# Four adj products and a W2 product in 128-wide tiles; three of the adj passes and the W2 product rewritten as one level of Strassen's seven products

## What is computed

```
def _gc(x, adj, W, b):
    return adj @ (x @ W) + b
h = jnp.maximum(_layernorm(x, axis=-1), 0.0)
h = jax.nn.relu(_gc(h, adj, W1, b1))
h = jax.nn.relu(_gc(h, adj, W2, b2))
return x + _gc(h, adj, W3, b3)
```

## Time and profile before

| | us |
|---|---|
| median of 3 runs (1734.08 to 1735.21) | 1734.35 |
| span of the profiled execution, from its first to its last instruction | 1732.1 |
| TensorE busy (matmul) | 1717.0 (99%) |
| VectorE busy | 628.4 (36%) |
| ScalarE busy | 451.6 (26%) |
| GpSimd busy | 43.8 (3%) |
| mean DMA rate | 110 GB/s |

### The profile page before, as it was taken

How to read it: one execution, slowest core, us unless ns; L and a number is a source line. 1 busy time by engine, 2 the same in 40 slices (tenths; PEclk the granted TensorE clock), 3 DMA queues, 4 the chain that set the end, 5 groups by cost and what they waited for, 6 DMA issues and landing times.

```text
span 1732.1 us, 23105 instructions
## 1 busy us (share of the span) xinstructions
PE 1717.0 (99%) x8352; PEld 1480.0 (85%) x8352; DVE 628.4 (36%) x1040; ACT 451.6 (26%) x829; POOL 43.8 (3%) x115
## 2 busy tenths in 40 slices
PE   7999999999999999999999999999999999999999
PEld 6788889988888899888888899888898888888899
DVE  7623333463332333653233353222233332333232
ACT  6522222332221222332222242111012322222221
POOL 6400000000000000000000000000000000000000
PEclk9999999999999999999999999999999999999999
DMA  5633333024443342133344365332253324444342
GB/s 187 190 94 102 97 97 83 9 62 119 124 116 105 107 128 70 32 105 113 108 121 120 100 188 146 95 96 85 84 154 106 98 87 136 143 147 122 105 123 86
DMA packets 133485, 190.17 MB, mean 110 GB/s; under 512 B 14938, under 2 KB 64698, under 8 KB 133422
## 3 DMA queue, kind: packets, MB, share of 16 engines
q1 hardware_dynamic: 99450, 161.39, 32.5%
q10 hardware_dynamic: 33972, 27.98, 4.9%
HBM read 161.34 MB, written 27.73 MB: 109 GB/s over the span
## 4 chain that ended last, share of the span: by engine, by line
PE 96%; DMA 1%; DVE 1%; POOL 1%; ACT 1%; issue 0%; ACTq 0%; DVEq 0%; SPq 0%
PE ps L867 32%; PE ps L868 32%; PE ps L869 32%; DMA stage<-x 1%; PE ps L891 1%; DVE stats L712 0%; DVE still_lo L543 0%; POOL spread L835 0%; POOL spread L833 0%; POOL spread L843 0%; DVE slot_lo L551 0%; ACT stage L678 0%; ACT still_hi L506 0%; ACT slot_hi L530 0%; DVE moments L714 0%
## 5 line engine op out<-in xcount | busy, mean ns | idle before, releaser
L867 PE MATMUL ps<-slot_hi,still_hi 128*128 128x512 f32 (+2 forms) x2016 | 735.1, 365 | 11.4 <-DVE still_lo L543 11.4
L868 PE MATMUL ps<-slot_lo,still_hi 128*128 128x512 f32 (+2 forms) x2016 | 734.3, 364 | 0.0
L869 PE MATMUL ps<-slot_hi,still_lo 128*128 128x512 f32 (+2 forms) x2016 | 734.0, 364 | 0.0
L551 DVE TENSOR_TENSOR slot_lo<-raw,slot_hi 128x512 fp32r<-128x512 f32 (+2 forms) x588 | 362.8, 631 | 752.0 <-ACT slot_hi L530 751.5
L530 ACT CAST slot_hi<-raw 128x512 fp32r<-128x512 f32 (+2 forms) x588 | 328.5, 573 | 1056.5 <-PE ps L869 784.1
L867 PEld LDWEIGHTS ps<-slot_hi,still_hi 128*128 128x128 f32 x2016 | 379.8, 188 | 65.4 <-DVE still_lo L543 12.4
L868 PEld LDWEIGHTS ps<-slot_lo,still_hi 128*128 128x128 f32 x2016 | 379.9, 188 | 53.0
L869 PEld LDWEIGHTS ps<-slot_hi,still_lo 128*128 128x128 f32 x2016 | 379.6, 188 | 53.1
L867 PE MATMUL ps<-W_hi,slot_hi 128*128 128x512 f32 x336 | 132.1, 393 | 0.0
L868 PE MATMUL ps<-W_lo,slot_hi 128*128 128x512 f32 x336 | 132.1, 393 | 0.0
L869 PE MATMUL ps<-W_hi,slot_lo 128*128 128x512 f32 x336 | 132.1, 393 | 0.0
(11 more groups left out here) (63 smaller groups left out, 563.4 us busy)
## 6 DMA issues: line engine op xcount, KB each, us to landing
raw<-adjT SPq DMA_DIRECT2D x336, 256.0 KB, 2.7
raw<-adjT SPq DMA_DIRECT2D x84, 192.0 KB, 2.4
raw<-adjT SPq DMA_DIRECT2D x84, 138.0 KB, 2.1
raw<-H SPq DMA_DIRECT2D x42, 256.0 KB, 2.9
raw<-W SPq DMA_DIRECT2D x32, 256.0 KB, 3.1
P<-stage ACTq DMA_DIRECT2D x32, 256.0 KB, 2.1
raw<-P SPq DMA_DIRECT2D x32, 256.0 KB, 2.7
H<-stage ACTq DMA_DIRECT2D x32, 256.0 KB, 2.3
```

Source lines behind the costliest of these rows:

```text
L551: dve.tensor_tensor(lo, src, hi.bitcast(F32), ALU.subtract).then_inc(lo_done, 1)
L867: pe.matmul(out, st_hi, mv_hi, start=start, stop=False)
L868: pe.matmul(out, st_hi, mv_lo, start=False, stop=False)
L869: return pe.matmul(out, st_lo, mv_hi, start=False, stop=stop)
```

## The change

The kernel is written anew; what is computed is the same. Its parts:

1. **Strassen.** `pass2a`, `pass2b`, `pass3` and `w2` each become one level of Strassen's scheme (seven products of half-size matrices in place of eight). For adj, 20 of the 21 full row blocks are paired (t, t + 10; `PAIRS` = 10) and the columns are split in halves of 1356 (`HALF`). The block 20 and the short one stay outside the scheme and are added as ordinary products (`left`, `slot_tail`). One group is one of the seven products (`part` 0 to 6), or the left-over one (`None`), for one chunk: ten moving tiles, each multiplied by two stationary column blocks, 6 matmuls a tile.
2. **Width.** The padded 2712 columns are 2 halves of 3 chunks of 452 (`W` = 452). `pass1` stays an ordinary product, in 3 chunks of 2 x 452 columns, over eight PSUM banks.
3. **Combined moving operands.** Four of the seven products need sums of adj blocks (T1 to T4). GpSimd makes them during `pass1` from the raw tiles, four operations per pair of tiles (`make`, L1258), 3 x 10 pairs in all, and SP stores them to DRAM (`TS`); later passes load them in place of adj. For `w2` GpSimd makes them from `P2` (`prep_moving`, L1344), with loads and stores on its own DMA queue.
4. **Combined stationary operands.** S1 to S4 are made by GpSimd from each finished pair of h1 (`combine`, L1297) for `pass2a` and `pass3`; for `pass2b` and `w2` GpSimd makes them from DRAM during `pass2a` (`prep_stationary`, L1321).
5. **Reloading.** All stationary operands (10 pairs x 7 parts) fill one array `S`. h1's second half goes to DRAM (`H1B`), and `S` is loaded and cut again for `pass2b` and for `w2` while the pass before is running: one 128 x 256 tile beside each moving tile, through the same raw buffers.
6. **Drains.** PSUM banks are added into SBUF sums (`parts`) by VectorE, 2 to 4 additions a group; ScalarE copies part 0.
7. **Buffers.** `RAW` and `RING` go from 7 to 5, x buffers from 4 to 3 (`XS`); `pass1` has 5 raw and 3 cut slots of 904 columns.
8. h1's two halves are made in one phase. P1 goes to DRAM and back. The final x is added by GpSimd. The code has no loops any more: TensorE's program goes from 4473 to 7670 rows.

The core of the diff:

```diff
-RING = 7
-RAW = 7
-STAGES = 4
-CHUNK_BLOCKS = (4, 4, 4, 4, 3, 2)
+PAIRS = 10
+W = 452
+CHUNKS = 3
+HALF = W * CHUNKS
+RING = 5
+RAW = 5
+XS = 3
+LAG = 5
...
+            def make(i, which):
...
+                    pool.tensor_tensor(T1_, Y12, Y11, ALU.subtract).then_inc(made_done, 1)
...
+                    pool.tensor_tensor(T3_, Y22, Y12, ALU.subtract).then_inc(made_done, 1)
...
+                    pool.tensor_tensor(T2_, Y22, T1_, ALU.subtract).then_inc(made_done, 1)
...
+                    pool.tensor_tensor(T4_, Y21, T2_, ALU.subtract).then_inc(made_done, 1)
...
+            for g_n, part in enumerate((0, 1, 2, 3, None, 4, 5, 6)):
...
+                if reload and c == CHUNKS - 1 and part is not None and part >= 2:
+                    extra = reload(part - 2, last_of)
...
+                    if half is not None and (t == here[0] if here else True):
+                        p.tails += 1
+                        g.tail = (p.tails, c, half, at["tail_freed"])
+                        at["tail_freed"] = g.done[-1]
+                        p.steps.append(("tail", g))
+                    spread_in(extra)
...
+                if n >= XS:
+                    sp.wait_ge(lo1_done, xs1[n - XS].ready)
...
+                    for m in range(2):
+                        cols = slice(m * P, (m + 1) * P)
+                        if n == 0:
+                            bank_free(g, m)
+                        end = g.left is None and n == len(g.tiles) - 1
+                        mm = three(ps[:, g.banks[m], 0:W], S[:, j.pair, j.part, 0, cols], S[:, j.pair, j.part, 1, cols],
+                                   ring[:, s, 0, 0:W], ring[:, s, 1, 0:W], start=n == 0, stop=end)
```

More of the change, by code:

```diff
@@ L37 @@
 BANK = 512
-RING = 7
-RAW = 7
-HEAD = 4
-LATE = 4
-STAGES = 4
-STEP = 32
-EPS = 1e-5
-CHUNK_BLOCKS = (4, 4, 4, 4, 3, 2)
-def chunk_of(block):
-    at = 0
-    for c, n in enumerate(CHUNK_BLOCKS):
-        at += n
-        if block < at:
-            return c
-    return len(CHUNK_BLOCKS) - 1
-class Job:
-    def __init__(self, kind, cut, chunk=0, tile=0, col=0, width=0, half=None, source=None):
+EPS = 1e-5
+STEP = 32
+PAIRS = 10
+FULL = 21
+SHORT = 21
+ORDER = (1, 2, 3, 4, 5, 6, 0, 7, 8, 9)
+EARLY = 8
@@ new lines, with __init__ @@
+BLOCKS = [b for t in ORDER for b in (t, t + PAIRS)] + [20, SHORT]
+W = 452
+CHUNKS = 3
+HALF = W * CHUNKS
+NP = 2 * HALF
+DIRECT = {0: (0, 0), 1: (1, 0), 6: (1, 1)}
+X11, X12, S2, S3, S1, X22, S4 = range(7)
+RING = 5
+RAW = 5
+RAW1 = 5
+RING1 = 3
+XS = 3
+LAG = 5
+class Tile:
+    def __init__(self, kind, cut):
+        self.kind, self.cut = kind, cut
+        self.raw = self.raw_freed = self.slot = None
+        self.block = self.part = self.pair = self.chunk = self.half = self.k = None
+        self.freed = self.place_freed = None
@@ L68, in __init__, with columns_chunk @@
+def columns_chunk(block):
+    first = block * P
+    last = min(first + P, 2 * HALF) - 1
+    return max((c % HALF) // W for c in range(first, last + 1))
+class Pass1Tile:
+    def __init__(self, kind, cut):
         self.kind, self.cut, self.ready = kind, cut, cut + 1
-        self.chunk, self.tile, self.col, self.width, self.half, self.source = chunk, tile, col, width, half, source
-        self.raw = self.raw_freed = self.tail_use = self.slot = self.acc_before = self.slot_before = None
+        self.raw = self.raw_freed = self.pair_freed = self.slot = None
+        self.freed = self.place_freed = None
+        self.chunk = self.block = self.n = self.k = self.col = None
@@ L297, in gcn_kernel @@
[L297 to L306 removed]
+        assert offset + size <= nc.sbuf_usable_end, (name, offset + size - nc.sbuf_usable_end)
@@ L367, in source_of @@
[L367 to L383 removed]
+        copied = sem("copied")
```

1986 lines of the change are left out of this document (1271 added, 715 removed).

## The result

The changed kernel takes 1772.51 us (median of 4 runs, 1769.16 to 1774.82), the one before 1734.78 us beside it; the ratio is 1.0218, with a 95% interval of 1.0202 to 1.0233. It is slower by 2.2%, where I had forecast 1657 us and given 0.05 to slower.

A forecast was written before the change was run, and what follows sets the result against it. TensorE's count of matmuls was taken to bound the kernel. From 1732.1 us, -136.5 for columns, +32 reload, +8 first chunk and +18.9 in smaller waits (2.4 + 5 + 2 + 7 + 2.5) gave 1654.5, or 1657 as measured; range 1612 to 1718.

The forecast's parts named there:

- The count of columns: TensorE's matmuls in the passes and `w2`: fewer columns to multiply would save 136.5 us in sum.
- 452 columns are 68 above 384: Matmul time at the new width, taken from a line between 384 and 512 columns: 0.2017 us.
- Costed at nothing: GpSimd's preparation queue: GpSimd's making of combined operands, taken as covered by the rest of `pass2a`; uncovered, some 6 us each.
- once a landing takes over 4.7 us, five buffers no longer cover: Raw buffers in the passes: threshold of 2.56 + 2.1 us landing time, above which TensorE waits.
- the rival of 0.05: Slower landings decide all through the passes: at 6.3 us each, 206 us more, 1863 us; chance 0.05.
- the mean rate, about doubled: Load rate in the passes: DMA engines, busy 0.36 of the time at 99 GB/s, would fit it doubled.
- The clock: TensorE's granted clock, read as 1.00 (2.4 GHz) in every stretch before; no term was given for a change.
- Reload: Stretches with a 256-column tile behind each moving one: 1.50 us a pair against 1.21, +32 us (bounds 9 and 96).
- The first chunk: Load of x no longer hides with three buffers: 5.3 us a block against 4.84, +8 us (bounds 0 and 35).
- That rival (0.24): GpSimd and VectorE shut each other out, in the first chunk and reload stretches: 1712 us; chance 0.24.
- the seams: Waits between phases and at short tiles: +2.4 us after `pass1`, +5 into `pass2a`, +2 into `pass3`, +7 at short tiles.
- The end: After the last matmul, VectorE, GpSimd's addition and the store follow one another: +2.5 us.

## Why the prediction was wrong

The forecast span was 1654.5 us, the measured one 1770.8. The 116 us, by the forecast's own steps (the differences are rounded):

| step | forecast | measured | difference |
|---|---|---|---|
| start of the first matmul | 9.5 | 10.5 | +1 |
| 5076 matmuls at 0.2017, 1536 in `pass1` | 1333.6 | 0.2067 and 0.2048: 1363.8 | +30 |
| block phases | 242.9 | 240.8 | -2 |
| first chunk, TensorE idle | 6.8 + 8 | 26.6 | +12 |
| rest of `pass1`, with the seam | 2.4 | 7.3 | +5 |
| chunks with preparation and no reload (first two of `pass2a`, second of `pass2b`) | 5 + 2.3 | 29.3 | +22 |
| three reload stretches | 32 + 2.3 | 67.5 | +33 |
| first chunk of `w2` | 0 | 5.4 | +5 |
| `pass3` | 2 + 2.3 | 8.1 | +4 |
| end, after the last matmul | 5.4 | 11.9 | +6 |

**The count of columns** (-136.5) was mis-sized: the saving is 106. The step that failed is "452 columns are 68 above 384", a straight line between two measured widths. The run with TensorE alone shows that it is the width, and not what runs beside it; the operand's place adds up to 2 ns. "TensorE: Matmul & The Clock Gate" of the Trainium skill, whose rule I had weighed (N/2.4 + 2.5 ns), gives 190.8 ns; no run here shows 452 columns under 204.

**"Costed at nothing: GpSimd's preparation queue"** is the step that failed outright. I asked only whether it would be done in time, not what its transfers and additions do to the tiles beside them. Leaving it out gives 48.6 us back, 30.2 by its transfers (5.4 of them at the end) and 18.4 by its additions. My own threshold, "once a landing takes over 4.7 us, five buffers no longer cover", was about right and was reached in part: the median landing was 4.5 to 4.7 us in the second chunk of `pass2a` (11.3 us of stalls) and 3.7 to 4.0 in the second of `pass2b` (4.2 us), against 2.8 to 3.3 without preparation. I had made it the rival of 0.05 for all passes at once; it came true in stretches. And I had taken the mean rate, about doubled, as harmless, where it was the landing time under that rate that counted.

**The clock** was a term put at nothing without a word: I had read 1.00 in every stretch before and carried it over. The stalls brought TensorE to 1.2 GHz eleven times, some 16 of the 116 us, which stand in the table with the stalls behind which they came.

**Reload** (+32, bounds 9 to 96) had the right formula and a short landing: 3.1 to 3.4 us in place of 2.56 for the moving tiles, 2.8 to 2.9 in place of 2.1. That alone makes (4.6 + 3.8) / 5 = 1.68 us a pair instead of 1.50. Without preparation the three stretches keep 49.3 us of stalls; the 18 us above are preparation's again, 6 of them by the clock, which fell four times in these stretches and, with the preparation left out, not once.

**The first chunk** (+8, bounds 0 to 35) had the right cause, that x has one buffer less, and too short a block: 5.3 us forecast, while the statistics start 6.3 us apart ((74.44 - 55.56) / 3):

```profile
55.56 0.69 DVE L1046 BATCH_NORM_STATS2 stats<-xs 128x6 f32<-128x512 f32 x1 [2.96 <-DMA xs<-x]
74.44 0.69 DVE L1046 BATCH_NORM_STATS2 stats<-xs 128x6 f32<-128x512 f32 x1 [2.61 <-DMA xs<-x]
```

What was missing is the mutual waiting of GpSimd and VectorE: 1.4 to 2.0 us for about every second cut, which takes 1.08 alone, and `lo` often at 1.63 instead of 0.75. That rival (0.24) was real in kind, and is a smaller part than the missing buffer. It also contributes in the passes, where VectorE's 452-column rows take 743 ns beside preparation against 628 alone.

**Right were** the seams: the largest single stalls are 2.8 us after `pass1` (2.4 forecast), 5.3 into `pass2a` (5), 2.5 into `pass3` (2), 0.95 at each short tile (0.78); that plain chunks stall at nothing else; and ScalarE waiting for the DMA in the reload stretches. The end was missed: not the addition, which costs 1.1 us each, but GpSimd's drain, with whose late work the tail is 6.3 us longer than without it.

The chances were wrong in their shape. Most of the mechanisms that came true stood in the text, and I let each go wrong alone. In the passes they share one cause, the tile interval halved from 2.72 to 1.24 us over fewer buffers, and so they came together.

## What to carry to other kernels

When a change halves the work per tile, what decides is (landing + handling) / buffers against the new interval, with the landing as it is beside all the new traffic, background transfers included; before this one I would count the buffers (seven before, five after) first of all. Work put on an idle engine "for free" has a price in the transfers it makes late and in the SBUF inputs it shares with VectorE; leave it out once and read what it costs. Measure the width you mean to use; do not draw a line between two others.
